# One-hots of four chunks of edges in one 16-bit comparison, two short target spans per group, and reordered hand-overs, in a four-layer graph kernel

## The reference

```
adj0[src, dst] = 1; adj0[dst, src] = 1; adj0 += eye            # layer 0, 0/1, symmetric
x = layernorm(x + D^-1/2 adj0 D^-1/2 (x @ W0) + b0)
h = three GCN convolutions: segment_sum(norm * (x @ W)[src], dst) + b   # layer 1, edge counts
x = layernorm(x + h)
x = layernorm(x + softmax(mask(q k^T / sqrt(512))) v)          # layer 2, 0/1 mask from the edges
x = layernorm(x + two GCN convolutions with a relu between)    # layer 3
```

## Time and profile before

| what | us |
|---|---|
| median of 3 runs | 595.64 (594.64 to 596.05) |
| the profiled execution's own time | 594.13 |
| its span, first to last instruction | 592.3 |
| counting, first to last chunk (15.48 to 124.51) | 109.03 |
| from the last chunk to `rows_step(0)` (124.51 to 144.59) | 20.08 |
| `rows_step(0)` to the last product (144.59 to 586.5) | 441.9 |
| behind the last product | 5.8 |

### The profile page before, as it was taken

One profiled execution on the slowest core, in us unless ns is written; L12 is line 12 of the kernel. 1 busy time (PEld: TensorE's weight loads), 2 busy tenths in 40 slices (PEclk: granted clock), 3 DMA queues, 4 the chain that ended last, 5 costly groups with the idle time before them and its releaser, 6 DMA issues.

```text
span 592.3 us, 6470 instructions
## 1 busy us (share of the span) xinstructions
PE 575.1 (97%) x2113; PEld 342.4 (58%) x2113; DVE 298.0 (50%) x825; ACT 174.4 (29%) x360; POOL 103.3 (17%) x112
## 2 busy tenths in 40 slices
PE   3999999999999999999999999999999999999996
PEld 3555655555787844888744544444444487458742
DVE  5999899948678124234593102333334430450065
ACT  2898688737011121111011111111114102110200
POOL 3000000007433600000160002023333180000012
PEclk9999999999999999999999999999999999999998
DMA  8614000000100000000040000000000000000012
GB/s 302 214 57 157 1 0 2 1 1 2 37 4 2 0 1 0 0 1 0 1 160 0 1 0 0 1 0 1 0 0 1 3 0 1 0 0 1 0 54 89
DMA packets 9238, 16.20 MB, mean 27 GB/s; under 512 B 1507, under 2 KB 1523, under 8 KB 9206
## 3 DMA queue, kind: packets, MB, share of 16 engines
q1 hardware_dynamic: 9206, 15.75, 7.8%
HBM read 13.64 MB, written 2.11 MB: 27 GB/s over the span
## 4 chain that ended last, share of the span: by engine, by line
PE 93%; DVE 3%; issue 1%; ACT 1%; POOL 1%; DMA 0%; POOLq 0%; DVEq 0%; SPq 0%; ACTq 0%
PE bank L646 18%; PE bank L602 15%; PE bank L585 12%; PE bank L747 9%; PE bank L767 9%; PE bank L514 6%; PE bank L488 5%; PE bank L735 5%; PE bank L496 2%; PE bank L461 2%; PE bank L492 2%; PE bank L757 1%; PE bank L453 1%; PE bank L474 1%; DVE xs L1082 1%
## 5 line engine op out<-in xcount | busy, mean ns | idle before, releaser
L400 POOL TENSOR_TENSOR rstd<-veps,mhalf 128x1 f32<-128x1 f32 x32 | 23.9, 748 | 302.6 <-DVE veps L1075 302.6
L996 DVE TENSOR_SCALAR hot_key<-col_key,keyed 128x320 bf16<-128x320 int16 x256 | 64.6, 292 | 0.1
L747 PE MATMUL bank<-xt,tt 128*128 128x512 f32 x128 | 56.1, 592 | 0.0
L767 PE MATMUL bank<-vv,probt 128*128 128x512 f32 x128 | 56.1, 592 | 0.0
L646 PE MATMUL bank<-v_sb,gt 128*128 128x512 f32 x128 | 55.3, 592 | 0.0
L602 PE MATMUL bank<-adj,y_hi 128*128 128x512 f32 x128 | 51.3, 401 | 0.0
L602 PE MATMUL bank<-adj,y_lo 128*128 128x512 f32 x128 | 50.5, 395 | 0.0
L514 PEld LDWEIGHTS bank<-hot_key,hot_lo 128*128 128x128 bf16 x256 | 25.0, 98 | 38.6 <-issue 16.0
L514 PE MATMUL bank<-hot_key,hot_lo 128*128 128x320 bf16 x256 | 45.5, 299 | 0.0
L1082 DVE SCALAR_TENSOR_TENSOR xs<-bank,dinv,xs 128x512 f32<-128x512 f32 x24 | 17.7, 748 | 53.9 <-PE bank L646 38.3
L833 ACT ACTIVATE apart<-col_lo,edge_key 128x128 bf16<-128x128 int16 x128 | 43.8, 391 | 0.0
(11 more groups left out here) (174 smaller groups left out, 939.4 us busy)
## 6 DMA issues: line engine op xcount, KB each, us to landing
w_sb<-in_L_gnn_W_dram SPq DMA_DIRECT2D x3, 1024.0 KB, 5.3
xs<-in_x_dram SPq DMA_DIRECT2D x2, 1024.0 KB, 7.8
v_sb<-in_L_gnn_W_dram SPq DMA_DIRECT2D x2, 1024.0 KB, 6.8
out_dram<-xs SPq DMA_DIRECT2D x8, 256.0 KB, 2.0
w_sb<-in_L_gnn_weight_dram SPq DMA_DIRECT2D x1, 1024.0 KB, 8.1
wq_sb<-in_L_gnn_Wq_dram SPq DMA_DIRECT2D x1, 1024.0 KB, 12.1
wk_sb<-in_L_gnn_Wk_dram SPq DMA_DIRECT2D x1, 1024.0 KB, 13.6
wv_sb<-in_L_gnn_Wv_dram SPq DMA_DIRECT2D x1, 1024.0 KB, 7.4
```

The costliest lines, as they stand in the source:

```text
L747: mm = pe.matmul(bank[:, 2 * (i % 2) + c, :], tt[:, k, i * P:(i + 1) * P], xt[:, k, c * D:(c + 1) * D], start=k == 0, stop=k == FB - 1)
L767: mm = pe.matmul(bank[:, 6 + i % 2, :], probt[:, i % 2, j, :], vv[:, j, :], start=j == 0, stop=j == NB - 1)
L996: V.tensor_scalar(hot_key[:, slot * CPG + c, :], col_key[:], keyed[:, 0, bass.ds(g + c * G, 1)], None, ALU.is_equal).then_inc(hot_set, 1)
```

## The change

In the counting:

- The tables are interleaved: `hot_key[slot]` is now (key, chunk) with the chunk innermost, and one `tensor_tensor` comparison of `col_key` (int16, each key four times) with `key16` (int16, the four chunks' keys of the group, repeated along the keys by a step of 0) makes all four at once. `lo_near` is the same for VectorE's two `lo` tables. TensorE reads a chunk's table at every fourth 16-bit element, and `lo_near` at every second.
- The window is 24 targets for each pair of chunks, with a base of its own. A chunk's product has 8 x 24 = 192 columns, the two pairs of a group lie side by side in a bank, and VectorE adds two windows of 192 per group, the tables of a later group between them.
- The keys are `h*4096 + (dst - base - shift)`, so keys out of the window match nothing, and the set-up shrinks from eight instructions to three. ScalarE takes over two conversions at the start and the copy of `edge_key`, and its function table is loaded by a dummy copy at the start.
- SHARE is 1400 in place of 1300.

Elsewhere: VectorE clears 5 of the 8 blocks of `count` and GpSimd 3 (GpSimd all before); W0 comes in four DMAs with a semaphore each; `low` sits behind sym h = 2 to 5 in place of 3 to 6; TensorE's two branches are swapped (`If(big < 1)` first, so the path taken follows on in memory); `normalise(NB + 3)` of layer 1 comes ahead of the residual of block 4; and the last 128 rows are multiplied, added, normalised and stored in two halves of 256 columns.

```diff
-WIN = 40
+WIN = 24
+PAIR = 2
...
-SHARE = 1300
+SHARE = 1400
...
-        hot_lo = at("hot_lo", at_adj, [P, SLOTS * CPG, P], BF16)
-        hot_key = at("hot_key", at_adj + SLOTS * CPG * P * 2, [P, SLOTS * CPG, KEYS], BF16)
+        lo_near = at("lo_near", at_adj, [P, SLOTS, P, BY_DVE], BF16)
+        lo_far = at("lo_far", at_adj + SLOTS * BY_DVE * P * 2, [P, SLOTS, CPG - BY_DVE, P], BF16)
+        hot_key = at("hot_key", at_adj + SLOTS * CPG * P * 2, [P, SLOTS, KEYS, CPG], BF16)
...
-                    sp.dma_start(w0_sb[:], wview(w0)).then_inc(w_in["0"], 16)
+                    for k in range(FB):
+                        sp.dma_start(w0_sb[:, k, :], w0[k * P:(k + 1) * P, :]).then_inc(w0_in[k], 16)
...
-            nc.gpsimd.memset(count[:].bitcast(F32), 0.0).then_inc(const_set, 1)
+            nc.gpsimd.memset(count[:, ZEROED:NB, :].bitcast(F32), 0.0).then_inc(const_set, 1)
...
-            def chunk(at_hot, at_bank, c):
-                return pe.matmul(bank[:, at_bank, 0:KEYS], hot_lo[:, at_hot, :], hot_key[:, at_hot, :],
-                                 start=c == 0, stop=c == CPG - 1)
+                mm.then_inc(rows_turned, 1)
+            pe.wait_ge(rows_set, 2)
+            pe.matmul(bank[:, 0, 0:2 * SPANS * G], ones[0:G, :], group_dia[:].rearrange("g a b -> g (a b)"),
+                      start=True, stop=True).then_inc(rows_turned, 1)
+
+            def chunk(slot, c):
+                span = slice(c // PAIR * KEYS, (c // PAIR + 1) * KEYS)
+                lo = lo_near[:, slot, :, c] if c < BY_DVE else lo_far[:, slot, c - BY_DVE, :]
+                return pe.matmul(bank[:, slot, span], lo, hot_key[:, slot, :, c],
+                                 start=c % PAIR == 0, stop=c % PAIR == PAIR - 1)
...
+                    for cols in (low_cols, high_cols) if (s, b) == (23, HALF - 1) else (slice(0, D),):
+                        for k in range(FB):
+                            if b == 0:
+                                pe.wait_ge(*freed(g_from, k))
+                            if cols is high_cols:
+                                pe.wait_ge(*freed(22, 0))
+                            mm = pe.matmul(bank[:, 0 if cols is high_cols else HALF * (s % 2) + b, cols],
+                                           g(k, j), w[:, k, cols], start=k == 0, stop=k == FB - 1)
+                        mm.then_inc(hs_done, 1)
...
-            with pe.If(big > 0):
+            with pe.If(big < 1):
+                layer1([adj])
+            with pe.Else():
                 layer1([adj, rest_l1])
-            with pe.Else():
-                layer1([adj])
...
+            nc.scalar.copy(esum[:, 0, 0:1], ones[:, 0:1])
+            act.wait_ge(bits_set, 1)
+            nc.scalar.copy(key_rows[:, 0, :], bits[:, 0, :]).then_inc(act_rows_set, 1)
+            act.wait_ge(bits_set, 2)
+            nc.scalar.mul(key_rows[:, 1, :], bits[:, 1, :], float(APART)).then_inc(act_rows_set, 1)
+            act.wait_ge(rows_turned, 2)
+            nc.scalar.copy(edge_key[:, 0:2, :].rearrange("p a g -> p (a g)"), bank[:, 2, :]).then_inc(edge_set, 1)
...
+            then(V.memset(count[:, 0:ZEROED, :].bitcast(F32), 0.0))
...
-            def one_hots(g, slot, chunks=range(CPG)):
-
-                for c in chunks:
-                    if c < BY_DVE:
-                        V.tensor_scalar(hot_lo[:, slot * CPG + c, :], col_lo[:],
-                                        edge_key[:, 0, bass.ds(g + c * G, 1)], None, ALU.is_equal)
-                    V.tensor_scalar(hot_key[:, slot * CPG + c, :], col_key[:],
-                                    keyed[:, 0, bass.ds(g + c * G, 1)], None, ALU.is_equal).then_inc(hot_set, 1)
-
-            def windows_at(g):
-
-                _, values = nc.values_load_multi_w_load_instructions(
-                    base_at[0:1, bass.ds(g, BODY)], engines=[mybir.EngineType.DVE], min_val=0, max_val=N,
-                    skip_runtime_bounds_check_because="the table's entries are clamped to [0, N] when it is written")
-                return values
-
-            def add_window(at_dst, seen, slot):
+            def one_hots(g, slot):
+
+                V.tensor_tensor(lo_near[:, slot], col_near[:],
+                                lo16[:, bass.ds(g, 1), :].to_broadcast([P, P, BY_DVE]), ALU.is_equal)
+                V.tensor_tensor(hot_key[:, slot], col_key[:],
+                                key16[:, bass.ds(g, 1), :].to_broadcast([P, KEYS, CPG]), ALU.is_equal).then_inc(hot_set, 1)
...
+            def add_span(at_dst, slot, n):
+
+                return V.tensor_tensor(count[:, :, bass.ds(at_dst, WIN)],
+                                       bank[:, slot, n * KEYS:(n + 1) * KEYS].rearrange("p (h d) -> p h d", h=NB),
+                                       count[:, :, bass.ds(at_dst, WIN)], ALU.add)
...
+            def one_group(g, at_dst, seen, slot, ahead):
                 dve.wait_ge(win_summed, seen + 1)
                 dve.wait_ge(win_added, seen + 2)
-                V.tensor_tensor(count[:, :, bass.ds(at_dst, WIN)],
-                                bank[:, slot, 0:KEYS].rearrange("p (h d) -> p h d", h=NB),
-                                count[:, :, bass.ds(at_dst, WIN)], ALU.add).then_inc(win_added, 1)
-
-            SETUP = 8
+                add_span(at_dst[0], slot, 0).then_inc(span_added, 1)
+                if ahead is not None:
+                    one_hots(ahead, (slot + AHEAD) % SLOTS)
+                dve.wait_ge(span_added, seen + 1)
+                add_span(at_dst[1], slot, 1).then_inc(win_added, 1)
...
-                after(V.tensor_scalar(keyed[:, 1, :], edge_key[:, 2, :], shift[:], None, ALU.subtract), 1)
-                after(V.tensor_scalar(keyed[:, 0, :], keyed[:, 1, :], 0.0, FAR, ALU.is_lt, ALU.mult), 2)
-                after(V.tensor_scalar(keyed[:, 2, :], keyed[:, 1, :], float(WIN), FAR, ALU.is_ge, ALU.mult), 3)
-                after(V.tensor_tensor(keyed[:, 0, :], keyed[:, 0, :], keyed[:, 2, :], ALU.add), 4)
-                after(V.tensor_tensor(keyed[:, 0, :], keyed[:, 0, :], keyed[:, 1, :], ALU.add), 5)
-                after(V.tensor_tensor(keyed[:, 0, :], keyed[:, 0, :], edge_key[:, 1, :], ALU.add), 6)
-                after(V.tensor_scalar(base_at[:], group_row[0:1, 0, :], shift[0:1, :], float(N), ALU.add, ALU.min), 7)
-                after(V.tensor_scalar(shift[:], shift[:], float(WIN), None, ALU.add), 8)
+                after(V.tensor_scalar(key16[:].rearrange("p g c -> p c g"), keyed[:].rearrange("p (c g) -> p c g", c=CPG),
+                                      shift[:], None, ALU.subtract), 1)
+                after(V.tensor_scalar(base_at[:], group_row[0:1, 0, :], shift[0:1, :], float(N), ALU.add, ALU.min), 2)
+                after(V.tensor_scalar(shift[:], shift[:], float(WIN), None, ALU.add), 3)
...
-                if 3 <= h < 3 + HALF:
-                    low(h - 3, ya, xw[:, h - 3, :], dinv[:, 0, h - 3:h - 2])
+                if 2 <= h < 2 + HALF:
+                    low(h - 2, ya, xw[:, h - 2, :], dinv[:, 0, h - 2:h - 1])
...
+                if j == HALF:
+                    normalise(NB + HALF - 1)
                 residual(NB + j, 8 + j // HALF, NB, 1)
-                if j >= 1:
+                if j % HALF:
...
+            normalise(4 * NB - 2)
+            j = NB - 1
+            dve.wait_ge(biased, 3 * NB)
+            for n, cols in enumerate((low_cols, high_cols)):
+                dve.wait_ge(hs_done, 24 * HALF + n)
+                V.scalar_tensor_tensor(out=xs[:, j, cols], in0=bank[:, (NB - 1, 0)[n], cols], scalar=dinv[:, 1, j:j + 1],
+                                       in1=xs[:, j, cols], op0=ALU.mult, op1=ALU.add).then_inc(dve_out, 1)
+                dve.wait_ge(dve_out, freed(23, HALF - 1)[1] + n)
+                ins = V.bn_stats(stats2[:, n, :], xs[:, j, cols])
+            then(ins)
+            then(V.bn_aggr(mv[:, j, :], stats2[:].rearrange("p n s -> p (n s)")))
+            V.tensor_scalar(veps[:, j:j + 1], mv[:, j, 1:2], EPS, None, ALU.add).then_inc(var_set, 1)
+            dve.wait_ge(rstd_set, 4 * NB)
+            for cols in (low_cols, high_cols):
+                V.tensor_scalar(xs[:, j, cols], xs[:, j, cols], mv[:, j, 0:1], rstd[:, j:j + 1],
+                                ALU.subtract, ALU.mult).then_inc(normed, 1)
```

156 lines of the change are left out of this document (92 added, 64 removed).

## The result

| | before | after |
|---|---|---|
| median, us | 595.14 (593.97 to 596.05) | 609.32 (609.05 to 609.67) |
| span of the profiled execution | 592.3 | 607.2 |

The changed kernel takes 1.024 times as long, 95% interval 1.0219 to 1.0261: 14.2 us slower, where 12 us faster was forecast.

What follows compares the result with a forecast made beforehand. TensorE was taken to set the counting, with VectorE 8% behind. Terms -6.6 - 2.1 - 1.9 - 0.8 - 0.7 + 0 = -12.1 gave 583.5 us against 595.64, range 580 to 587.5.

Steps and rivals of the forecast that it cites:

- start: Ahead of the first chunk: table load and set-up instructions leave the way, -1.9 us, between -0.8 and -3.
- counting: TensorE's counting: shorter chunks -13.6, moved pieces +6.0, tight places +1.0, in all -6.6 us.
- branch: Ahead of layer 1's first product: the taken path falls through without a jump, -0.8 us, between 0 and -1.3.
- `normalise`: Ahead of layer 2's transposes: the early normalise removes a wait, -0.7 us, between 0 and -0.9.
- the paragraph on the chunks: Counting: 192 columns for 320, read at every fourth 16-bit element for free, save 0.21 us per group, -13.6.
- Rival 2: Counting: TensorE reads interleaved tables slowly, 0.16 us per chunk, 604.7; sign turns at 0.13 per chunk; chance 0.07.
- SHARE: Seven pieces move from behind the counting into it: +6.0 us there, only 2.1 coming back behind it.
- Rival 4: Start, jump and normalise give a third, or pauses between turns lower TensorE's clock: some +3.5, 587; chance 0.07.
- VectorE's group: Counting: VectorE's comparisons and windows take 1.44 us per group, under TensorE's 1.51; ends 1.2 and 1.98.
- rival 1: Counting: VectorE becomes the bound, comparisons at one result per cycle, group 1.98, 607.8 us; chance 0.07.
- The +1.0 for tight places: Counting: what VectorE and ScalarE cost TensorE in tight places, +1.0 us, between 0 and +3.5.
- Rival 3: Counting: only the strided weights are slow, two of four chunks at 0.109 us, +3.3, 586.8; chance 0.08.

Runs made afterwards that it cites:

- kernel 12: Kernel 6 (pairs, SHARE 1300, count cleared on VectorE) with SHARE 1200: 587.77 us, ratio to before 0.988.
- kernel 1: Changed kernel, but TensorE reads each chunk's 192 key columns from neighbouring elements (counts then wrong): 588.71 us, ratio to before 0.9894.
- kernel 9: Changed kernel, but TensorE reads its columns at every third 16-bit element (6 bytes): 597.54 us in one execution.
- kernel 4: Changed kernel with SHARE back at 1300: 603.46 us, 1.0119 to 1.0161 times before.
- with pairs: Changed kernel with key tables interleaved by two chunks, not four, so a chunk's columns are 4 bytes apart: 588.73 us.
- kernel 2: Changed kernel, but the weights of VectorE's two lo tables load from neighbouring elements (counts then wrong): 609.49 us, 1.0222 to 1.0269 times before.
- kernel 3: Changed kernel with the key table interleaved by pairs of chunks in place of fours (step of 4 bytes): 588.73 us, 0.9877 to 0.9913 times before.
- 10: Changed kernel, but TensorE reads 96 columns at every eighth 16-bit element (16 bytes), twice over: 662.04 us in one execution.
- kernel 5: Changed kernel with tables interleaved by pairs and SHARE back at 1300: 583.32 us, ratio to before 0.98.
- kernel 6: Kernel 5 with all of count cleared on VectorE, none on GpSimd: 582.15 us, ratio to before 0.9777.
- 7: Kernel before with only the bodies of layer 1's branch on TensorE swapped: 592.73 us, ratio 0.997.
- 8: Kernel before with only layer 1's normalise of block 3 moved ahead of block 4's residual: 593.31 us, ratio 0.9983.
- 11: Kernel 6 with the bodies of layer 1's branch put back as before, early normalise kept: 580.97 us, ratio to before 0.977.

## Why the prediction was wrong, step by step

The forecast's span was 582.0 - 1.8 = 580.2; it is 607.2, 27.0 more. By its terms:

| term | forecast | measured | off by |
|---|---|---|---|
| start | -1.9 | +0.8 | 2.7 |
| counting | -6.6 | +15.0 | 21.6 |
| behind the counting | -2.1 | +0.4 | 2.5 |
| branch | -0.8 | -1.45 | -0.65 |
| `normalise` | -0.7 | +0.1 | 0.8 |
| end | 0 | +0.1 | 0.1 |

**What bounds it** was read rightly: TensorE sets the counting, and in kernel 12 VectorE does in the groups where TensorE needs less than 1.43.

**The step that failed** is in the paragraph on the chunks: "I take free: f32 operands, whose elements are 4 bytes apart, feed the same engine in the neighbouring rows; 8 bytes apart is one step further." That step doubles the read. By the chunks that is 256 x (0.167 - 0.083) = 21.5 us; kernel 1, which takes the step away, gives back 20.8 of the 21.6, and the other 0.8 is tight places (below). The row named as support didn't carry it: its f32 records take 0.43 us for 512 columns, 0.84 ns each, twice the 0.42 of the bf16 chunks beside them, so it doesn't show that even 4 bytes apart is free, and it says nothing of 8. No row ahead of the run did, as the prediction says; it had worked out both ends. Rival 2 is what happened, at its own 0.16 per chunk. Its turning point of 0.13 per chunk supposed that the other terms give what was forecast; since they fell short, kernel 9, with 0.128, is already above before (597.54 in one execution, against 595.43).

**SHARE**: the 6.0 that enter the counting are about right (5.9 in kernel 4, 5.2 with pairs). The 2.1 that should come back did not: with pairs, SHARE 1400 has 20.76 behind the counting and 1300 has 20.10. In all six profiles with SHARE 1400 (the changed kernel and 1, 2, 3, 9, 10) the clock falls among the last turns or in `g`, `g` takes 5.1 to 5.8, and the stretch is 19.97 to 20.97, by how early the clock fell. In six with 1300 (before, 5, 6, 7, 8, 11) the clock stays at 1.00 and the stretch is 20.07 to 20.10; only kernel 4 lost the clock, elsewhere. The times of `sym` were right: the last turn was expected 13.9 behind the last chunk and began at 154.51 - 140.27 = 14.24. What was missing is the clock. The turn then lasted 0.96 instead of 0.45, and `g` 5.24 instead of 3.52: 17.9 + 0.34 + 0.51 + 1.72 = 20.47, and 20.44 was measured. Rival 4 had this half of the mechanism with a chance of 0.07.

**VectorE's group** was right in each part, rival 1 is out. **The +1.0 for tight places** was +1.8 in kernel 1 (103.20 against 101.4), within its bounds.

**Start**: the five set-up instructions and the table load did go. The GpSimd side was left out: an iota of 768 takes 2.38 us, the clearing 1.41 more, and VectorE's first instruction on the edges stood until both were done. Moving the clearing gave 1.35 of the 2.7. Where the other 1.35 lies was not tried; in kernel 6 VectorE begins `bits` at 5.25, behind its own clearing and the iota, where kernel 5's began at 4.06, so its own clearing may have cost it most of that.

**Branch and `normalise`**: each term was too small alone (1.4 for 0.8, 0.9 for 0.7), and the sum too large together. "The jump at the body's end now lies ahead of a wait" was true with the branch alone; the second edit removed that wait. Two edits on one gap don't add. That the pause belongs to the jump is argued from where it comes and goes (kernels 7, 8, 11); no row names it. Rival 3 fell with kernel 3, whose near and far chunks take the same 0.17 per two. **The end** was right.

Kernel 5 takes 583.32 us, near the forecast of 583.5. That is luck: it has the pairs and the SHARE of before, its first chunk is 2.7 later than forecast, and its counting is 10.5 shorter than before, not 6.6.

## What to carry to other kernels

When one instruction can build several tables by interleaving them, look at who reads them: on TensorE the moving operand of this kernel was free up to a step of 4 bytes and cost in proportion beyond, so two 16-bit tables can be interleaved and not four. Work that fills TensorE's pauses between short products can be worth more than its own time: without it the clock fell in six profiles of six, and `g` took 5.1 to 5.8 us for 3.5. Before taking such work away, price the rest at 1.2 GHz. It is no guarantee, as in kernel 4 the clock fell where TensorE had no pause. And before summing the gains of two edits, check whether one of them was the cover of the other.

## What the runs showed of the hardware that I had not expected

- TensorE's moving operand: 192 bf16 columns take 0.085 us at steps of 2 and 4 bytes, 0.128 at 6, 0.167 at 8, 0.33 at 16. Weights at a step of 4 bytes cost nothing more, at 0.085 (kernel 3) as at 0.167 (kernel 2).
- The granted clock fell to 0.50 in the fourth of a row of pauses of 0.54, 0.52, 0.53 and 1.45 us with turns of 0.6 between them (the changed kernel), and in kernels 4 and 10 with no pause at all.
- A VectorE instruction on int32 in SBUF lasted 2.45 us (the changed kernel) and 3.01 (kernel 5) instead of 0.40 while GpSimd ran an iota and a memset.
- An iota of 768 elements that repeats each value four times took 2.38 us, 3.1 ns an element.
- Beside a branch that TensorE takes there stood a pause of 0.2 to 1.4 us, of different size in programs that are alike around it. That the branch makes it is argued, not shown.
